# A windowed attention stack: the mask is added by VectorE on the way from PSUM to SBUF instead of by TensorE products

## The reference

```
mask = (it < jb) | (it > jb + w) | (jb == -1)
sim = jnp.einsum('bhwie,bhwje->bhwij', bq, bk2) * QK_SCALE
sim = jnp.where(mask, -jnp.finfo(sim.dtype).max, sim)
attn = jax.nn.softmax(sim, -1)
out = jnp.einsum('bhwij,bhwje->bhwie', attn, bv2)
```

## Time and profile before

| | us |
|---|---|
| median of 3 runs | 3917.49 |
| lowest and highest | 3913.91, 3923.57 |
| profiled execution, whole | 3918.71 |
| its span, first to last instruction | 3916.9 |

### The profile page before, as it was taken

How to read it: one execution, slowest core, us unless ns; L and a number is a source line. 1 busy time by engine, 2 the same in 40 slices (tenths; PEclk the granted TensorE clock), 3 DMA queues, 4 the chain that set the end, 5 groups by cost and what they waited for, 6 DMA issues and landing times.

```text
span 3916.9 us, 146395 instructions
## 1 busy us (share of the span) xinstructions
PE 3581.4 (91%) x60128; PEld 2226.2 (57%) x60128; DVE 3162.1 (81%) x4377; ACT 2652.5 (68%) x4972; POOL 2432.0 (62%) x2197
## 2 busy tenths in 40 slices
PE   5676776899999999999999999999999999999997
PEld 2222222566666666666666666666666666666664
DVE  4899998888878778888878788778787887888884
ACT  3555554677777777767776777677777777676765
POOL 0355554876666666666666666666666666666661
PEclk9889898999999999999999999999999999999999
DMA  3000000111111111111110111111111111110101
GB/s 76 0 0 0 0 0 0 34 32 31 31 42 41 34 30 31 31 47 38 35 32 26 42 42 36 32 31 31 45 37 33 31 31 47 36 36 27 32 28 37
DMA packets 64418, 120.05 MB, mean 31 GB/s; under 512 B 18196, under 2 KB 35986, under 8 KB 63634
## 3 DMA queue, kind: packets, MB, share of 16 engines
q1 hardware_dynamic: 63762, 110.70, 9.7%
HBM read 20.50 MB, written 2.10 MB: 6 GB/s over the span
## 4 chain that ended last, share of the span: by engine, by line
PE 53%; DVE 15%; issue 9%; ACT 7%; POOL 0%; ACTq 0%; DMA 0%; DVEq 0%; POOLq 0%; SPq 0%
PE ob L1187 10%; PE qk L1129 9%; PE sc L1214 7%; PE trb L1001 6%; PE vob L1195 4%; PE vob L1135 4%; PE sc L1163 4%; DVE arena L888 3%; PE sc L1221 3%; DVE ssq L894 3%; DVE mx L901 3%; PE ob L1001 2%; DVE arena L889 2%; ACT arena L619 2%; DVE xnT L978 1%
## 5 line engine op out<-in xcount | busy, mean ns | idle before, releaser
L507 POOL TENSOR_TENSOR arena<-arena,rnorm 128x512 f32<-128x512 f32 x768 | 793.7, 1054 | 929.3 <-ACT rnorm L626 928.8
L500 POOL TENSOR_TENSOR arena<-arena 128x512 f32<-128x512 f32 x768 | 961.7, 1274 | 84.9 <-DVE arena L889 84.9
L633 ACT ACTIVATE arena<-trb 128x512 f32<-128x512 f32 x768 | 465.7, 606 | 432.4 <-PE trb L1001 432.4
L1129 PE MATMUL qk<-wqkv,xs 128*128 128x512 f32 x1536 | 734.2, 601 | 16.0 <-issue 8.9
L888 DVE TENSOR_TENSOR arena<-qk,tab_q 128x512 f32<-128x512 f32 x384 | 263.7, 687 | 504.6 <-ACT arena L619 499.6
L483 POOL TENSOR_TENSOR arena<-arena 128x512 f32<-128x512 f32 x256 | 299.9, 1180 | 345.4 <-DVE arena L858 329.9
L1001 PE MATMUL trb<-ident,arena 128*128 128x128 f32 x3072 | 483.0, 280 | 10.7 <-ACT arena L633 7.6
L619 ACT ACTIVATE arena<-qk 128x512 f32<-128x512 f32 x768 | 433.5, 592 | 79.4 <-PE qk L1129 65.5
L1129 PEld LDWEIGHTS qk<-wqkv,xs 128*128 128x128 f32 x1536 | 294.5, 193 | 312.0 <-issue 294.8
L894 DVE TENSOR_REDUCE ssq<-arena 128x16 f32<-128x1024 f32 x384 | 464.3, 1209 | 0.0
L514 POOL TENSOR_TENSOR arena<-arena,rinv 128x512 f32<-128x512 f32 x384 | 392.4, 1043 | 65.8 <-DVE rinv L911 65.8
(11 more groups left out here) (139 smaller groups left out, 6020.5 us busy)
## 6 DMA issues: line engine op xcount, KB each, us to landing
arena<-arena SPq DMA_DIRECT2D x192, 384.0 KB, 3.2
arena<-arena SPq DMA_DIRECT2D x192, 64.0 KB, 3.0
wqkv<-in_L_ffn_Wqkv SPq DMA_DIRECT2D x18, 512.0 KB, 4.3
wo<-in_L_ffn_Wo SPq DMA_DIRECT2D x6, 512.0 KB, 4.0
arena<-in_L_attn_x SPq DMA_DIRECT2D x8, 256.0 KB, 2.8
out<-arena SPq DMA_DIRECT2D x8, 256.0 KB, 2.2
w<-in_L_ffn_W SPq DMA_DIRECT2D x6, 341.0 KB, 2.9
arena<-in_sel SPq DMA_DIRECT2D x1, 1024.0 KB, 5.0
```

Source lines behind the costliest of these rows:

```text
L500: nc.gpsimd.tensor_tensor(ts[c * 2 + j][:, heads], tu[:, 0, heads], tu[:, 1, heads], ALU.add).then_inc(summed[0], 1)
L507: nc.gpsimd.tensor_tensor(part, part, rnorm[j][:, 8 * h:8 * h + 8].unsqueeze(2).to_broadcast([P, 8, HEAD]), ALU.mult) \
L633: A((qT, kT)[j][u][:, 4 * h:4 * h + 4, at_col:at_col + P], TRB.rearrange("p (a t) -> p a t", a=4), ACT.Copy) \
L1129: MM(QK[:, 512 * h:512 * h + 512], lhsT=xs[u][:, c * P:(c + 1) * P], rhs=wqkv[:, col:col + 512], start=True, stop=True) \
```

## The change

VectorE's first pass over the scores becomes an addition: SC plus mask, out of PSUM into the SBUF tile prob. The mask tile is read again for each of the 8 column blocks of 128. The maximum is then taken over prob, and the subtraction works in place in prob. The wait for prob to be free (pt_done) moves ahead of the addition. A new semaphore, masked, is given by the addition; PE waits for it where it waited for sub_done (before the scores, the up and the down products). PE's two mask products a step are gone, the score products write with start=True, and PE adds one semaphore increment (s_open) ahead of them. ACT's exps still waits for sub_done, which lost its initial credit.

```diff
         def _(dve):
             V = nc.vector
             give_credits(dve, [x_kept, ln_xc, ln_out, bc_split, dbx_done, scan_done, y_skip, mo_used,
-                               ssq_done, roped, sub_done, x_next, conv_done])
+                               ssq_done, roped, masked, x_next, conv_done])
...
             def maxima(s, B, u, j, n):
                 item(dve, s_done, s)
-                scores = SC[:, :].rearrange("p (h t) -> p h t", t=SPAN)
-                V.reduce_max(mx[n % 2][:], scores, AX.X).then_inc(mx_done[0], 1)
                 slot(dve, pt_done, s * 2 + 1)
+                V.tensor_tensor(prob[n % 2].rearrange("p (q b) t -> p q (b t)", b=2), SC[:, :].rearrange("p (q t) -> p q t", t=2 * SPAN),
+                                mask[:, :].unsqueeze(1).to_broadcast([P, STEP_HEADS, 2 * SPAN]), ALU.add).then_inc(masked[0], 1)
+                item(dve, masked, s)
+                V.reduce_max(mx[n % 2][:], prob[n % 2], AX.X).then_inc(mx_done[0], 1)
                 dve.wait_ge(mx_done[0], s + 1)
-                V.tensor_tensor(prob[n % 2], scores, mx[n % 2][:, :].unsqueeze(2).to_broadcast([P, 2 * STEP_HEADS, SPAN]), ALU.subtract) \
+                V.tensor_tensor(prob[n % 2], prob[n % 2], mx[n % 2][:, :].unsqueeze(2).to_broadcast([P, 2 * STEP_HEADS, SPAN]), ALU.subtract) \
                     .then_inc(sub_done[0], 1)
...
             def scores(s, B, u, j, n, up0, up1, up2, down):
 
                 item(pe, tr_evac, B * (2 * UNITS) + (2 * UNITS - 2 + j))
-                slot(pe, sub_done, s)
+                slot(pe, masked, s)
...
-                for h in range(2):
-                    MM(SC[:, 512 * h:512 * h + 512], lhsT=ident16[:], rhs=mask[:, :].unsqueeze(1).to_broadcast([P, STEP_PAIRS, 2 * SPAN]),
-                       start=True, stop=True)
+                pe.sem_inc(s_open[0], 1)
                 for a in range(STEP_PAIRS):
                     for b, g, t0 in windows():
                         for h in range(2):
                             d, col = slice(64 * h, 64 * h + 64), 512 * h + a * 2 * SPAN + b * SPAN
                             last = MM(SC[32 * g:32 * g + 32, col:col + SPAN], lhsT=qT[u][d, STEP_PAIRS * j + a, t0:t0 + WINDOW],
-                                      rhs=kT[u][d, STEP_PAIRS * j + a, t0:t0 + SPAN], start=False, stop=True, skip_group_check=True)
+                                      rhs=kT[u][d, STEP_PAIRS * j + a, t0:t0 + SPAN], start=True, stop=True, skip_group_check=True)
                 last.then_inc(s_done[0], 1)
...
                 if scored:
-                    item(pe, sub_done, scored[0])
+                    item(pe, masked, scored[0])
```

More of the change, by code:

```diff
@@ L300, in build @@
         vs_in = sem("vs_in")
+        s_open = sem("s_open")
         s_done = sem("s_done", 2 * STEPS)
         mx_done = sem("mx_done")
-        sub_done = sem("sub_done", 1)
+        masked = sem("masked", 1)
+        sub_done = sem("sub_done")
         exp_done = sem("exp_done")
```

## The result

The changed kernel takes 4090.23 us in the median of four runs (4088.88 to 4092.08), the kernel before 3916.15 (3913.91 to 3923.57): ratio 1.0441, 95% interval 1.0423 to 1.0459. It is slower, by 174 us. The forecast was 4095, with 4035 to 4160 as its range.

What follows compares the result with a forecast made beforehand. VectorE's chain through the block of maxima was taken to bound most stretches, not PE at 91%. 0.87 + 1.32 + 0.11 + 1.32 = 3.62 us a period, 46 times 166.5, plus 9.2 and 1, on 3918.7: 4095 us; range 4035 to 4160.

Steps and rivals of the forecast that it cites:

- What bounds the kernel: In each of four stretches the longer of VectorE's chain and PE's product row sets the time; PE waits in two.
- PE's gain a step, 0.43 to 0.53: Two mask products a step, 0.53 us, go; the s_open increment in their place takes 0 to 0.53, taken as 0.1.
- The block, +1.32: VectorE's passes from the first over the scores to square_sums grow from 2.46 to 3.78 us by one waited-for pass.
- Slots 2-3 and 6-7, +1.32 each: Mean product (waiting for add_x) and first up product (waiting for the norm's last pass) each start 1.32 us later.
- Slots 4-5, +0.11: Variance product: PE and VectorE were level; it starts 0.04 us later, plus 0.07 for restarting after a wait.
- Slots 0-1, +0.87: Second transposes wait for ACT's later copy out of TRB: +0.82 us, +0.87 with the restart.
- Rival A: ACT's chain in slots 0-1 isn't late, so that stretch gives -0.43: 2.32 us a period, 4036 us; chance 0.09.
- The first steps and the last: Seven steps ahead of the first norm add 9.2 us; the last three add between -1.5 and +4, taken as 1.
- Rival C, the clock: PE's clock falls to 1.2 GHz at each longer wait for the mean: 60 us lost, so 4155; chance 0.09.
- PE's clock unchanged: One of the signs listed as showing the forecast right: PE's clock does not change.
- Rival D: POOL's passes hold up VectorE's subtraction by 0.8 us in three stretches a period: 110 us more, 4205; chance 0.03.

Runs made afterwards that it cites:

- e1: The changed kernel with PE's two mask products a step put back, VectorE's addition and SBUF passes kept: ratio 1.0441 to the kernel before.
- e2: The kernel before without its mask products and with no mask added, so output not the reference's: 3874.95 us, ratio 0.9878.
- e9: The kernel before with one line moved, the wait for pt_done ahead of the maximum: 3918.28 us, ratio 0.9989.
- e6: The changed kernel with ACT's copy out of TRB ahead of table load and gelu in the second up pair's slot: ratio 1.0377 to the kernel before.
- e3: The kernel before without any mask, plus one extra VectorE pass over 512 of 1024 columns, overwritten afterwards: 3997.64 us, ratio 1.0182.
- e5: The changed kernel with the two passes ending the norm moved ahead of rope on VectorE: 4028.47 us, ratio 1.0275 to the kernel before.
- e4: The changed kernel with the third pair of up products issued ahead of the mean product on PE: 4063.16 us, ratio 1.0351 to the kernel before.
- e7: The changed kernel with the three order changes of e4, e5 and e6 together: 4009.49 us, ratio 1.0231 to the kernel before.

## Why the prediction was right

**What bounds the kernel.** That PE, at 91%, doesn't set two of the four stretches was the step on which all hung. e1 and e2 show it from both sides: PE's mask products are worth nothing that can be measured beside the longer block, and 0.43 us in two stretches beside the short one.

**PE's gain a step, 0.43 to 0.53.** It is 0.43 (e2), so what stands in place of the mask products, the increment of s_open in it, takes the 0.1 that was assumed.

**The block, +1.32.** This term was mis-sized; it is +1.19. The passes were priced well (1.21, 1.22, 1.22 us against 1.23, 1.21 and 1.24). What failed is "a pass whose result is waited for takes 1.32 from start to start": that row held a second wait, which the change takes out of the chain. The trace of before had the right pair in sums and reciprocal (L909 at 2057.91, L911 at 2059.16: 1.25), and the prediction didn't use it. 1.19 is also what the rule of the Trainium skill gave ("VectorE: DVE Perf Modes", section on the TRN2 errata), but not for its reason, in these passes: maximum and subtraction took 1216 and 1225 ns from PSUM and take 1220 and 1225 ns from SBUF, so the 65 ns a pass are not to be seen here, and e9 gets the short distance with both on PSUM.

**Slots 2-3 and 6-7, +1.32 each.** Measured +1.12 and +1.11 where the clock holds. The mechanism and the place are as told, with the block at 1.19. With the mask products kept (e1) both stretches grow by the whole block, 1.19 and 1.21; the prediction took PE's gain as nothing here, and dropping the products gave 0.06 and 0.11. The waits are 2.67 and 1.71 against the 3.1 and 2 told: the block is shorter by 0.13, and before the mean PE's gain lengthened the wait by only 0.22 (e2: 1.48 against 1.26), not by 0.43.

**Slots 4-5, +0.11.** Measured -0.03 to -0.04: with 1.19 in the place of 1.32 the product starts earlier by 0.13. The new wait for add_x is there, 0.15, not 0.5.

**Slots 0-1, +0.87.** Measured +0.67, through ACT's copy out of TRB as told (the wait reads 1.03; 1.3 was told). e6 takes the wait away and its stretch falls to PE's own 14.93. Rival A is out.

**The first steps and the last.** 7.3 for six steps against 9.2 for seven; 2.4 at the end against 1.

**Rival C, the clock, came true in part.** The forecast gave it 0.09 and argued that 3.1 us lies near the harmless row, 2.91. With a wait of 2.67 it fell in 16 of 47 turns and cost 27 us; a single row without a fall was no evidence that there is none, and "PE's clock unchanged", one of the prediction's own signs, did not hold. The price of a fall, 1.34 us, was somewhat low (1.69).

**So the sum was right for partly wrong reasons.** Without the clock a period grew by 2.87 us, not 3.62: 46 x 2.87 = 132, where 166 were forecast. 2.87 lies below the prediction's own range of 3.0 to 4.1 a period. The clock's 27 us and a few microseconds at layer changes filled most of the gap: without the 27 the time would have been about 4063, within the stated range of 4035 to 4160, but not near 4095. That it came within 5 us was luck: a block priced too long and a clock that the sum left out nearly cancelled.

**Rival D didn't come.** The subtraction, with two SBUF inputs, takes 1225 ns in the mean of 192, as before; POOL's passes were over, as argued: none overlaps one of the 192 subtractions. The rule on shared ports that the prediction cites was not put to the test.

**Open.** What decides in which turns the clock falls. Before the mean it fell behind waits of 2.0 us (e3) in 33 of 47 turns, 2.4 (e1) in 22, and 2.67 in 16 (changed kernel), 14 (e6) and 7 (e5), and in none behind 1.26 or 1.48. It did not fall at the first up product's wait of 1.71. But it fell in 3 turns of e4 behind 1.03, in 6 of e7 behind 1.13 to 1.15, and twice in the kernel before where PE had sat 1.12 us. So the length of the wait alone doesn't decide it: the share doesn't grow with the wait, it differs between kernels with the same wait, and no length above 1 us is shown to be safe everywhere. What else it hangs on is not worked out here.

## What to carry to other kernels

An engine at 91% need not set the time. Look in each stretch for which wait ends last, and put the new work's length on that chain, not on a sum of busy time. Work taken from the fullest engine is worth something only in stretches where that engine doesn't wait, and work given to another costs its length, less the slack of its chain, wherever something waits behind it in that engine's order: of the 1.19 us here 1.12 and 1.11 in two stretches, 0.67 in the third and nothing in the fourth. A wait taken away shows the next one, and only part of its length is won (e4, e6). Before pricing a chain by one distance from start to start, see which waits stand inside it and whether the change moves them.

## What the runs showed of the hardware that I had not expected

The granted clock of PE fell to 1.2 GHz for a good 3 us at waits of only 2.0 to 2.67 us between busy stretches, in 7 to 33 of 47 turns, at 1.7 us each; filling the wait with other products (e4) ended it at that place. It fell, more rarely, behind waits of 1.03 to 1.15 us too (e4, e7). A VectorE maximum, sum, addition or subtraction over 1024 fp32 columns took 1.21 to 1.23 us wherever its inputs lay, two SBUF tensors included, and with a bf16 second operand (L903, 1215 ns). One more semaphore wait between two dependent VectorE passes cost 0.07 us (1.32 against 1.25, e9 and 171 against 20 steps of the kernel before).
